# Stack layers: the band mask written to PSUM by eight 64-row, 32-column matmuls instead of two whole-array ones

## What is computed

```python
def local_attention(q, k, v):
    w = WINDOW                                   # 32
    ...                                          # windows of 32 queries; keys of this and the window before
    mask = (it < jb) | (it > jb + w) | (jb == -1)
    sim = jnp.einsum('bhwie,bhwje->bhwij', bq, bk2) * QK_SCALE
    sim = jnp.where(mask, -jnp.finfo(sim.dtype).max, sim)
    attn = jax.nn.softmax(sim, -1)
    out = jnp.einsum('bhwij,bhwje->bhwie', attn, bv2)
```

## Time and profile before

| | |
|---|---|
| median of 3 runs | 4463.43 us |
| lowest and highest | 4456.26 and 4473.81 us |
| profiled execution | 4466.84 us |
| its span, first to last instruction | 4465.1 us |
| mean granted TensorE clock | 0.972 |
| PE busy share of the span | 91% |
| DVE, ACT and POOL busy share | 74%, 52%, 56% |
| mask matmuls (L1080) | 384, in 192 slots |

### The profile page before, as it was taken

How to read it: one execution, slowest core, us unless ns; L and a number is a source line. 1 busy time by engine, 2 the same in 40 slices (tenths; PEclk the granted TensorE clock), 3 DMA queues, 4 the chain that set the end, 5 groups by cost and what they waited for, 6 DMA issues and landing times. The chain is left out here.

```text
span 4465.1 us, 195370 instructions
## 1 busy us (share of the span) xinstructions
PE 4085.3 (91%) x89528; PEld 2450.9 (55%) x89528; DVE 3289.0 (74%) x4385; ACT 2340.3 (52%) x3044; POOL 2496.9 (56%) x2036
## 2 busy tenths in 40 slices
PE   6887899999999999999678877999999999999997
PEld 2322666666666666666333335666666666666664
DVE  7997678777777877788454436777787777777774
ACT  6885455555555555555234443455555555555553
POOL 0002677776777767776200006677676776767673
PEclk8999899999999999999789998999999999999998
DMA  0001111111112112111000011112112111111110
GB/s 19 1 1 45 44 53 35 53 46 46 52 31 60 42 42 59 33 32 32 12 1 1 1 36 41 53 33 60 42 39 55 40 50 47 43 52 38 32 36 21
DMA packets 92028, 162.87 MB, mean 36 GB/s; under 512 B 33997, under 2 KB 55241, under 8 KB 91209
## 3 DMA queue, kind: packets, MB, share of 16 engines
q1 hardware_dynamic: 91208, 150.36, 12.4%
HBM read 48.61 MB, written 1.05 MB: 11 GB/s over the span
## 5 line engine op out<-in xcount | busy, mean ns | idle before, releaser
L1102 PEld LDWEIGHTS banks<-f_P_T,f_V_previous 32*64 32x64 f32 x24576 | 482.9, 131 | 509.6 <-issue 486.9
L1102 PE MATMUL banks<-f_P_T,f_V 32*64 32x32 f32 x24576 | 578.5, 223 | 35.7 <-issue 34.8
L1102 PE MATMUL banks<-f_P_T,f_V_previous 32*64 32x32 f32 x24576 | 570.0, 227 | 28.1 <-issue 24.6
L1072 PE MATMUL banks<-f_wqkv,H 128*128 128x512 f32 x1152 | 568.4, 617 | 17.0 <-DVE f_rope_bk L1395 9.5
L1341 POOL TENSOR_TENSOR f_q_rotated<-f_rope_aq,f_rope_bq 128x1024 f32<-128x1024 f32 x192 | 454.6, 2368 | 231.4 <-DVE f_rope_bq L1395 231.0
L1072 PE MATMUL banks<-f_wqkv,G 128*128 128x512 f32 x1152 | 554.0, 603 | 0.6
L1392 DVE TENSOR_TENSOR f_rope_aq<-banks,f_rope 128x1024 f32<-128x1024 f32 x192 | 235.2, 1225 | 429.6 <-ACT f_sqq L1254 415.0
L1341 POOL TENSOR_TENSOR f_k_rotated<-f_rope_ak,f_rope_bk 128x1024 f32<-128x1024 f32 x192 | 451.9, 2354 | 165.9 <-DVE f_rope_bk L1395 165.8
L1328 POOL MEMSET f_kT<- 128x256 f32 x2 | 0.6, 312 | 838.7 <-POOLq L514 460.8
L1102 PEld LDWEIGHTS banks<-f_P_T,f_V 32*64 32x64 f32 x24576 | 440.6, 133 | 41.7 <-issue 40.5
L1126 PE MATMUL banks<-f_O_T,f_wo 128*128 128x128 f32 x3072 | 437.6, 289 | 4.9 <-issue 4.9
(11 more groups left out here) (204 smaller groups left out, 8489.5 us busy)
## 6 DMA issues: line engine op xcount, KB each, us to landing
f_V_previous<-f_V SPq DMA_DIRECT2D x192, 384.0 KB, 3.6
f_V_previous<-f_V SPq DMA_DIRECT2D x192, 128.0 KB, 2.3
f_wqkv<-in_L_ffn_Wqkv SPq DMA_DIRECT2D x48, 384.0 KB, 4.1
f_rope<-in_rope SPq DMA_DIRECT2D x24, 512.0 KB, 5.2
f_wo<-in_L_ffn_Wo SPq DMA_DIRECT2D x12, 512.0 KB, 5.2
f_w<-in_L_ffn_W SPq DMA_DIRECT2D x12, 341.0 KB
f_w<-in_L_ffn_W SPq DMA_DIRECT2D x24, 64.0 KB
xin<-in_L_attn_a_x SPq DMA_DIRECT2D x2, 512.0 KB, 5.0
```

The costliest lines, as they stand in the source:

```text
L1072: mm = nc.tensor.matmul(ps[:, o * BLK:(o + 1) * BLK], xs, w[:, c * INNER + o * BLK:c * INNER + (o + 1) * BLK], start=True, stop=True)
L1102: mm = nc.tensor.matmul(banks[i * DH:(i + 1) * DH, g * BLK + k * W:g * BLK + (k + 1) * W], of[n % 3][r, h * DH:(h + 1) * DH], PT[n % 2][r, ...
```

## The change

The mask of a slot is written by eight matmuls instead of two. Each has 64 rows, 32 columns and the same 512 moving columns, so it has the array form of the scores that follow. All eight weights are the 32 x 32 identity with 32 rows of zeros. The mask gets a second copy of its first-window rows at partitions 64 to 95, and the variant is chosen for each window: only window 0 of a sequence's first tile takes the one with the masked keys. The matmuls stay bf16, and the waits stay where they were.

```diff
             def scores(n, t):
                 u = n % 2
                 pe.wait_ge(qT_ev.sem, qT_ev.at(n))
-                for i in range(2):
-                    nc.tensor.matmul(PT_S[:, i * BLK:(i + 1) * BLK], ident16[:],
-                                     mask[:, (1 if t else 0):(2 if t else 1), :].to_broadcast([P, HP, 2 * W]),
-                                     start=True, stop=False)
+                for g in range(NG):
+                    v = 1 if t or g else 0
+                    for i in range(2):
+                        rows = slice(i * DH, (i + 1) * DH)
+                        nc.tensor.matmul(PT_S[g * W:(g + 1) * W, i * BLK:(i + 1) * BLK], ident16[rows, i * DH:i * DH + W],
+                                         mask[rows, v:v + 1, :].to_broadcast([DH, HP, 2 * W]), start=True, stop=False)
                 pe.wait_ge(kT_ev.sem, kT_ev.at(n))
```

```diff
     band[:, :, :] = np.where((j < a) | (j > a + W), f(NEG), f(0))[:, None, :]
     band[0:W, 0, 0:W] = NEG
+    band[2 * W:3 * W, 0, 0:W] = NEG
```

## The result

The changed kernel takes 4448.4 us in the median of 16 runs (4437.7 to 4457.0) against 4463.5 us for the kernel before (16 runs, 4456.3 to 4473.8). The ratio is 0.9965 with a 95% interval from 0.9956 to 0.9974, so it is 15 us faster, a third of a per cent. A second series gave 0.9962 (0.9947 to 0.9978). The forecast was 4437 us.

The account below looks back on a forecast made before the run. TensorE's list of work was taken to bound the stack. 124 slots x 0.20 us (24.8) plus 48 GELU slots x 0.07 (3.4) made 28 us, less 2 is 26: 4437 us against the median 4463.43, range 4420 to 4463.

Parts of the forecast that it names:

- 22 to 32 us less: Whole kernel: the forecast's own case, around 26 us gained, chance 0.58.
- 0 to 8 us less: Whole kernel: little or nothing gets through, as DVE's rotation or POOL's chain is the limit; 4455 to 4463 us, chance 0.24.
- What bounds the kernel: In the stack, TensorE's list of work (busy 1361 of 1400 us), apart from short waits inside the slot.
- The two chains from the Q projection: In a slot: TensorE's own through mask, scores, V projection and copy of V; DVE's through the rotations, never passing the mask.
- What goes and what comes: Between K projection and scores: 0.52 us removed, 0.10 form change and 0.23 masks added; V projection 0.20 us earlier.
- The rival of serial masks: At the eight masks: two at a time gives 4546 us, one after the other 4705 us; slower, chance 0.08.
- that case at "about 0": At the masks: only four of eight overlap, two rounds eat the whole gain; about 4463 us, within little or nothing, 0.24.
- How much gets through: Behind the V projection: 0.20 us passes by the copy of V in most slots, 0.07 us in 48 GELU slots; 28 us.
- the 0.31 us read from the idle time: Before the feed-forward matmul: TensorE idle for the copy of V, slack said to cover the whole 0.20 us.
- one slot is typical: The slot read in the trace was called typical because all 384 mask matmuls have the same length, 379 ns.
- the 2 us taken off for all the rest: Over all slots: deducted from 28 us for slots that meet the next limit, such as POOL's normalised K.
- 124 slots: Of the 144 slots without a GELU, those where TensorE waits for the copy of V; x 0.20 us gives 24.8 us.

Follow-up runs that it names:

- mask_twice: The changed kernel with its eight mask matmuls written twice, the second eight accumulating; 4462.5 us, ratio 0.9998 to the kernel before.
- mask_64x128: The kernel before with its two mask matmuls on 64 rows and all 128 columns, one for each row half; 4449.0 us, ratio 0.9964.
- mask_128x32: The kernel before with eight mask matmuls of 128 rows and 32 columns, so only four tiles; 4478.4 us, ratio 1.0027.
- mask_thin: The changed kernel with mask matmuls of 64 moving columns instead of 512, same instruction list; 4448.8 us, ratio 0.9976 to the kernel before.
- no_mask: The changed kernel without the eight mask matmuls, scores starting on an empty bank; 4594.5 us, ratio 1.0289 to the kernel before.
- rot_short_after: The changed kernel with DVE's last product of the rotation of K on 8 of 16 heads; 4421.7 us, ratio 0.9907 to the kernel before.
- The edit of DVE's chain: DVE's last product of the rotation of K on 8 of 16 heads; 4446.4 us on the kernel before, 4421.7 us on the changed one.

## Why the prediction was right or wrong

The time lies in the range, and the change is faster, but by 15 us where the forecast had 26, and within the 0.5% beyond which it had put most of the chance. It lies between two of its cases, 22 to 32 us less and 0 to 8 us less, in neither. That the time is within the range is owed to the range's width, which held the case of no gain as well. By its own steps:

*What bounds the kernel.* Right. The two chains from the Q projection are there, the products with V did not move, and the copy of V carried the gain.

*What goes and what comes.* Right, and a little low. The change of form costs 0.09 us in its new place. The eight masks cost 0.23 us. `mask_twice` gives 0.21 us for a further round, and `mask_64x128` shows a second change of form at 0.10 us. I had 0.19 to 0.21 us for the V projection; it is 0.23. The 0.03 us missed are in the scores, whose 128 starts take 1.24 us instead of 1.27. The weight loads of the scores now begin while the masks still stream, which may be why; no run tests it. The six pairs more cost nothing in the slot. The Trainium skill's span rule (TensorE: Matmul & The Clock Gate, section The mechanism), with 4 ns a tile, gives 0.387 + 7 x 0.004 = 0.415 us for the block as an estimate; the trace has 0.41, and 3.3 ns between starts.

*The rival of serial masks.* Excluded, by the starts and by `mask_128x32`, which is that rival with four tiles at a time. I had put that case at "about 0"; with the second change of form it is 12 us slower.

*How much gets through.* The mechanism was right, and in undisturbed slots so were the sizes: 0.23 us in three of four, 0.05 instead of 0.07 in GELU slots. The room at the copy of V was larger than the 0.31 us read from the idle time, whose start is a modelled end of a matmul: `mask_thin`, with the products with V ending last, shows 10.22 - 9.84 = 0.38 us. (That one slot is typical did not follow from the equal lengths of the masks either, since a mask's length says nothing of the waits around it; it held for the sizes above, not for the pauses.) The term that failed is the 2 us taken off for all the rest. Adding up the distances between starts of matmuls in the 163 slots from 0.62 to 2.06 ms and from 2.86 to 4.32 ms (mean of two profiles each, after less before) gives this account:

| | us |
|---|---|
| V projection earlier, 163 x 0.23 | -37.5 |
| more waiting in front of the products with V, for DVE | +35.3 |
| first part of the products with V shorter, by fewer pauses | -6.9 |
| less waiting in front of the feed-forward matmuls, for the copy of V | -21.8 |
| second part of the products with V longer | +8.3 |
| more time lost in the scores, behind them, in the projections and elsewhere | +6.2 |
| sum | -16.4 |

The first four lines are the mechanism. They give 31 us, which is what undisturbed slots promise (122 x 0.23 + 41 x 0.05 = 30), and 36 us for 192 slots. The forecast had 28 there: 124 slots were too few rather than too many. The last two lines, 14.5 us, are what it put at 2 us. The second part of the products is the largest of them: 121.8 and 122.7 us before, 130.0 and 131.2 after. The difference is time without a semaphore: pauses over 0.1 us there add up to 17 us before and 25 after. Beyond these slots, the two profiles after have some 4 us more in the pipeline's two ends.

*Why more room does not help more.* Three kernels move the V projection forward by 0.11, 0.23 and 0.40 us (`mask_64x128`, the change, `mask_thin`). Their undisturbed slots are 0.11, 0.23 and 0.38 us shorter up to the feed-forward matmul, where no GELU is in the way. Their ratios are 0.9964, 0.9965 and 0.9976. By their undisturbed slots they would gain 18, 36 and 57 us; they gain 16, 15 and 11, with some 4 to 6 us either way. So the first 0.11 us pays almost in full, and what comes beyond brings nothing that can be seen. Pauses in the first part of the products with V do not explain it for the change: they add up to 14 us before, of which 13 fell into the room, and 7 after, of which 6 did, so about 1 us counts either way (4 of 6 us in `mask_thin`, where no room is left). The second part, which has no room behind it, tells more: 118, 131 and 139 us in the three kernels, against 122 before.

*What stays open.* That accounts for a part only. Why the second part's pauses grow was not tested on purpose, but the runs narrow it down. `mask_thin` and the change have the same instruction list, and still differ by 8 us there, so the 12 instructions more in each slot, which shift the packets' borders, aren't the whole of it. `mask_twice`, with 16 more again and its slots as long as before, has 120 us. What goes with the longer second part in all kernels but `no_mask` is how soon the feed-forward matmul follows the start of the first part: 0.93 us in the change and 0.78 in `mask_thin`, against 1.16 before, 1.05 in `mask_64x128`, 1.15 in `mask_twice` and 1.18 in `rot_short_after`, whose second part takes 121 us with the change's own list. So two bursts of small matmuls that lie closer together would run dry more often; that reading was not tested, and `no_mask` (0.78 us, 110 us) speaks against it or has its pauses elsewhere. The edit of DVE's chain, worth 22 to 25 us with either kernel though no undisturbed slot waits for it at the end, takes 7 us from the second part in the kernel before and 10 in the changed one, of 13 and 18 us in these slots. The rest of its worth was not settled. `no_mask` against `mask_thin` shows that 16 instructions a slot fewer can matter by 140 us, and `mask_twice` that 16 more need not.

## What to carry to other kernels

Write small products into PSUM on tiles that can stream side by side, in the array form of their neighbours: the change of form (0.10 us) is still paid only once, and eight tiles of 64 x 32 stream in the time of one, here 0.23 us for what took 0.43. When a stage gets shorter on the path that seems to set a pipeline's slot, count the room at every join behind it, and don't expect the total to follow the slot: 0.11 us a slot paid almost in full here, and 0.40 us paid no more than that. And before leaving work out to measure its price, keep the instruction list the same length: nearly the same array time was 0.9976 or 1.0289 of the kernel before, by sixteen instructions a slot.

## What the runs showed of the hardware

TensorE's instructions arrive in packets of 16 KB, one for 256 of them (9 packets for 2304 instructions), and a dense run of small matmuls can run dry: it pauses for up to 2.8 us, and goes on 1.4 us (1.24 to 1.55 in most cases) after a packet has landed. What that costs hangs on the instruction list: 145 us in sum in the scores in one kernel, 1 to 12 us in others with nearly the same work.

A change of array form cost 0.09 to 0.10 us wherever it stood: between the K projection and masks of 64 x 32, and on either side of masks of 64 x 128.

Behind a change of form the 128 score records start fast at first, 32 of them within 0.24 us (6.6 ns apart inside runs of eight), and then slower, 10.4 ns apart on average. A part of the products with V begins alike, 32 records within 0.24 us, and takes 0.40 us for the next 32. With eight masks of 0.39 us ahead of them the first 32 score records need 0.31 us, but all 128 only 1.24 instead of 1.27.

Pauses also cost clock. Without the mask, TensorE's clock was at 1.2 instead of 2.4 GHz for 109 us in the two bodies, against 5 us before; each of 18 such stretches between 0.62 and 2.2 ms began within 1.6 us of the end of a pause of over 1.5 us.
